# Relation rows made in a pipeline of two groups, all ahead of the carry of the spread attention sums

## The reference

```python
x = _layernorm(x + _L0_gnn_ref(x, src, dst), axis=-1)
x = _layernorm(x + _L1_gnn_ref(x, edge_index, L1_gnn_w, ...), axis=-1)
x = _layernorm(x + _L2_gnn_ref(x, ..., src, dst, edge_type_86), axis=-1)
x = _layernorm(x + _L3_gnn_ref(x, edge_weight, edge_index, 100000), axis=-1)
```

```python
c = w_comp[etype]                       # 86 x 16, one row per edge
xb = jnp.einsum('ei,bio->ebo', x, weight)
msg = jnp.einsum('eb,ebo->eo', c, xb)
y_hat = y @ A2_w.T + A2_b + rel_emb[etype]   # 86 x 32, one row per edge
```

## Time and profile before

| | us |
|---|---|
| median of 3 runs | 2744.0 |
| lowest, highest | 2743.14, 2745.68 |
| the profiled execution | 2745.77 |
| its span in the trace | 2744.0 |

### The profile page before, as it was taken

How to read it: one execution, slowest core, us unless ns; L and a number is a source line. 1 busy time by engine, 2 the same in 40 slices (tenths; PEclk the granted TensorE clock), 3 DMA queues, 4 the chain that set the end, 5 groups by cost and what they waited for, 6 DMA issues and landing times.

```text
span 2744.0 us, 24747 instructions
## 1 busy us (share of the span) xinstructions
PE 533.3 (19%) x3579; PEld 337.4 (12%) x3579; DVE 1927.4 (70%) x3512; ACT 625.0 (23%) x1417; POOL 1732.6 (63%) x1741
## 2 busy tenths in 40 slices
PE   5770000273000000000003032320255550000000
PEld 2330000273000000000003012220122220000000
DVE  7777888888835456546898476059888887587872
ACT  7982233131000000000003013441344430100000
POOL 6777777777567665646657776670566621717776
PEclk9995555597555555555556565555565655555555
DMA  6003333100112122221231201111000001200000
GB/s 229 13 12 91 97 96 100 33 13 13 61 12 34 11 25 28 21 18 72 57 66 22 63 11 9 57 23 48 7 8 8 8 4 52 21 2 10 9 9 9
DMA packets 100894, 101.68 MB, mean 37 GB/s; under 512 B 58169, under 2 KB 92649, under 8 KB 98929
## 3 DMA queue, kind: packets, MB, share of 16 engines
q0 software_dynamic: 53664, 20.91, 8.2%
q1 hardware_dynamic: 46864, 80.15, 8.1%
q10 hardware_dynamic: 320, 0.20, 0.0%
HBM read 38.06 MB, written 60.81 MB: 36 GB/s over the span
## 4 chain that ended last, share of the span: by engine, by line
DVE 36%; issue 21%; POOL 15%; DMA 9%; PE 6%; DVEq 3%; ACT 2%; ACTq 1%; POOLq 1%; SPq 0%
POOL ring L781 6%; POOL cring L477 3%; POOL out_dram L493 3%; DMA cring<-sums_by_list,cidx 2%; PE banks L2746 1%; POOL ring L874 1%; POOL attention_by_edge L881 1%; DVE RB L1259 1%; DVE banks L1100 1%; DVE banks L1090 1%; DVE SW L1096 1%; DVE SW L1095 1%; DVE SW L1105 1%; DVE SW L1383 1%; DVE banks L1084 1%
## 5 line engine op out<-in xcount | busy, mean ns | idle before, releaser
L493 POOL DMA_INDIRECT out_dram<-ring,ridx x196 | 210.3, 1073 | 128.5 <-DVE ridx L2214 68.4
L502 POOL DMA_INDIRECT XS<-in_x_dram,xsi x196 | 199.3, 1017 | 70.0 <-issue 62.2
L502 POOL DMA_INDIRECT SW<-node_table,srci x196 | 200.4, 1022 | 66.1 <-issue 66.1
L502 POOL DMA_INDIRECT XD<-in_x_dram,xdi x196 | 195.4, 997 | 62.7 <-issue 62.7
L900 POOL DMA_INDIRECT out_dram<-z4w,oidx x112 | 111.9, 999 | 126.8 <-ACT oidx L2467 98.1
L477 POOL DMA_INDIRECT cring<-sums_by_list,cidx x128 | 123.8, 967 | 101.7 <-issue 71.0
L2614 PE MATMUL banks<-tl,dcar 128*128 128x32 f32 (+1 forms) x14 | 4.4, 405 | 766.6 <-DVEq L1372 584.1
L2532 PE MATMUL banks<-YW 128*128 128x392 f16 x784 | 139.5, 331 | 46.1 <-ACT YW L2298 45.9
L781 POOL DMA_INDIRECT ring<-x_by_edge,aidx x96 | 102.3, 1066 | 49.6 <-issue 44.8
L781 POOL DMA_INDIRECT ring<-rgcn_table,aidx x56 | 61.8, 1103 | 109.6 <-DMA aidx<-rows 93.4
L2273 ACT ACT_TABLE_LOAD x22 | 28.2, 1283 | 399.7 <-DVEq L1060 399.7
(11 more groups left out here) (614 smaller groups left out, 3328.6 us busy)
## 6 DMA issues: line engine op xcount, KB each, us to landing
SW<-in_x_dram SPq DMA_DIRECT2D x20, 625.0 KB
out_dram<-SW SPq DMA_DIRECT2D x20, 625.0 KB
sums_by_list<-RB SPq DMA_DIRECT2D x2, 1800.0 KB
sums_by_edge<-RB SPq DMA_DIRECT2D x1, 3528.0 KB, 9.8
sums_by_list<-RB SPq DMA_DIRECT2D x2, 1600.0 KB
XS<-in_x_dram,xsi POOLq DMA_INDIRECT x196
list_values_by_edge<-RB SPq DMA_DIRECT2D x1, 3136.0 KB
attention_by_edge<-RB SPq DMA_DIRECT2D x1, 3136.0 KB
```

Source lines behind the costliest of these rows:

```text
L493: pool.indirect_dma_start(out=table, out_offset=off, in_=ring_row(h, j, w), in_offset=None, bounds_check=limit, oob_is_err=False).then_inc ...
L502: pool.indirect_dma_start(out=dest[:, t * w:(t + 1) * w], out_offset=None, in_=table, in_offset=bass.IndirectOffsetOnAxis(ap=idx[:, t:t + ...
```

## The change

The step of a row is cut in three on ACT (distances, one-hots, copy) and in two on PE (transposes, products). `bank[0]` and `bank[1]` are used by halves, one for even and one for odd groups, and the distances get a second buffer, `xs16[:, 0, :]`; there is still one `ohr`. PE makes the transposes of group g + 1 ahead of the products of group g; they wait for the distances of group g, the products for one-hots g and copy g - 1. ACT does distances g + 1, copy g, one-hots g + 1. Each loop now holds two groups, so that the halves are constants. The batches on PE are 8 rows, `scar`, 8 rows, `sbak`, 32 rows and the products of the last, `dbak`; nothing stands behind `dbak`.

```diff
-        off16, ohr = x16[:, 0, :], x16[:, 1, :].bitcast(BF16)
+        off16, ohr = (x16[:, 0, :], xs16[:, 0, :]), x16[:, 1, :].bitcast(BF16)
...
-        ROWS_AHEAD, ROWS_BEHIND = 4, 10
+        ROWS_AHEAD = 8
...
+        types_of = lambda b: bank[0][:, b * 256:(b + 1) * 256].bitcast(F16)
+        rows_of = lambda b: bank[1][:, b * 256:b * 256 + GT * RW]
...
-            with act.Fori(0, NG) as g:
-                relation_row(g)
+            row_distances(0, 0)
+            row_onehots(0, 0)
+            with act.Fori(0, NG // 2) as m:
+                for b in range(2):
+                    row_distances(m * 2 + (b + 1), 1 - b)
+                    row_copy(m * 2 + b, b)
+                    row_onehots(m * 2 + (b + 1), 1 - b)
+            row_copy(NG - 1, 0)
...
+            def row_types(g, b):
+
+                pe.wait_ge(s_rab, g + 0)
...
+            def row_products(g, b):
+
+                pe.wait_ge(s_rcp, g + 1)
+                pe.wait_ge(s_roh, g + 1)
...
+            def row_pairs(first, n):
+
+                with pe.Fori(0, n // 2) as m:
+                    for b in range(2):
+                        row_types(m * 2 + (first + b + 1), 1 - b)
+                        row_products(m * 2 + (first + b), b)
...
-            for link in (scar, sbak):
-                with pe.Fori(0, ROWS_AHEAD) as g:
-                    relation_row(g + (0 if link is scar else ROWS_AHEAD))
-                carry(link, D)
-            with pe.Fori(0, NG - 2 * ROWS_AHEAD - ROWS_BEHIND) as g:
-                relation_row(g + 2 * ROWS_AHEAD)
-            carry(dbak, D)
-            with pe.Fori(0, ROWS_BEHIND) as g:
-                relation_row(g + (NG - ROWS_BEHIND))
+            for k, link in enumerate((scar, sbak)):
+                row_pairs(ROWS_AHEAD * k, ROWS_AHEAD)
+                carry(link, D)
+            row_pairs(2 * ROWS_AHEAD, NG - 1 - 2 * ROWS_AHEAD)
+            row_products(NG - 1, 0)
+            carry(dbak, D)
```

More of the change, by code:

```diff
@@ L446, in load_edges @@
             queue.dma_start(tile[P - 1:P, 0:LASTV], edges_last(a)).then_inc(loaded, 16)
+        types_of = lambda b: bank[0][:, b * 256:(b + 1) * 256].bitcast(F16)
+        rows_of = lambda b: bank[1][:, b * 256:b * 256 + GT * RW]
+        assert ROWS_AHEAD % 2 == 0 and NG % 2 == 1
         def slot_count(n, i, h):
@@ L2443, in _, with row_distances, row_onehots, row_copy @@
                     A.activation(xt[:, b, :], bank[b][:, 0:P], ACT.Copy).then_inc(s_dxtc, 1)
-            def relation_row(g):
+            def row_distances(g, b):
                 act.wait_ge(s_ret, g + 1)
                 act.sem_inc(tick, 1)
-                A.activation(off16[:, :], bank[0][:, 0:256].bitcast(F16), ACT.Abs, bias=pneg[:, 0:1]).then_inc(s_rab, 1)
+                A.activation(off16[b], types_of(b), ACT.Abs, bias=pneg[:, 0:1]).then_inc(s_rab, 1)
+            def row_onehots(g, b):
                 act.wait_ge(s_rab, g + 1)
                 act.sem_inc(tick, 1)
-                A.activation(ohr[:, :], off16[:, :], ACT.Relu, scale=-1.0, bias=1.0).then_inc(s_roh, 1)
+                A.activation(ohr[:, :], off16[b], ACT.Relu, scale=-1.0, bias=1.0).then_inc(s_roh, 1)
+            def row_copy(g, b):
                 act.wait_ge(s_rmm, g + 1)
                 act.sem_inc(tick, 1)
-                A.activation(RB[:, bass.ds(g * (GT * RW), GT * RW)], bank[1][:, 0:GT * RW], ACT.Copy).then_inc(s_rcp, 1)
-            with act.Fori(0, NG) as g:
-                relation_row(g)
+                A.activation(RB[:, bass.ds(g * (GT * RW), GT * RW)], rows_of(b), ACT.Copy).then_inc(s_rcp, 1)
+            row_distances(0, 0)
[6 more added lines that the diff above has]
+            row_copy(NG - 1, 0)
             sq_2 = (sq_p[:, 0:RC * D], nxs[0][:, 0:RC * D])
@@ L2689, in _ @@
             pe.sem_inc(s_rcp, 1)
-            def relation_row(g):
-                pe.wait_ge(s_rcp, g + 1)
+            def row_types(g, b):
+                pe.wait_ge(s_rab, g + 0)
                 pe.sem_inc(tick, 1)
                 for c in range(GT):
-                    last = M.transpose(bank[0][:, 0:256].bitcast(F16)[:, c * P:(c + 1) * P],
+                    last = M.transpose(types_of(b)[:, c * P:(c + 1) * P],
                                        ety16[:, bass.ds(g * GT + c, 1)].to_broadcast([P, P]), ident_h[:, :])
                 last.then_inc(s_ret, 1)
+            def row_products(g, b):
+                pe.wait_ge(s_rcp, g + 1)
                 pe.wait_ge(s_roh, g + 1)
@@ L2700, in relation_row @@
                     for k in range(3):
-                        last = M.matmul(bank[1][:, c * RW:(c + 1) * RW], ohr[:, c * P:(c + 1) * P], rel3[:, k, :],
+                        last = M.matmul(rows_of(b)[:, c * RW:(c + 1) * RW], ohr[:, c * P:(c + 1) * P], rel3[:, k, :],
                                         start=k == 0, stop=k == 2)
                 last.then_inc(s_rmm, 1)
-            for link in (scar, sbak):
-                with pe.Fori(0, ROWS_AHEAD) as g:
-                    relation_row(g + (0 if link is scar else ROWS_AHEAD))
+            def row_pairs(first, n):
[3 more added lines that the diff above has]
+                        row_products(m * 2 + (first + b), b)
+            for c in range(GT):
+                last = M.transpose(types_of(0)[:, c * P:(c + 1) * P], ety16[:, c:c + 1].to_broadcast([P, P]),
+                                   ident_h[:, :])
+            last.then_inc(s_ret, 1)
+            for k, link in enumerate((scar, sbak)):
+                row_pairs(ROWS_AHEAD * k, ROWS_AHEAD)
                 carry(link, D)
-            with pe.Fori(0, NG - 2 * ROWS_AHEAD - ROWS_BEHIND) as g:
-                relation_row(g + 2 * ROWS_AHEAD)
+            row_pairs(2 * ROWS_AHEAD, NG - 1 - 2 * ROWS_AHEAD)
+            row_products(NG - 1, 0)
             carry(dbak, D)
-            with pe.Fori(0, ROWS_BEHIND) as g:
-                relation_row(g + (NG - ROWS_BEHIND))
             pe.wait_ge(s_grp, 1)
```

## The result

| | before | changed |
|---|---|---|
| median us | 2744.1 | 2718.4 |
| lowest, highest | 2743.14, 2745.68 | 2716.25, 2721.93 |
| the profiled execution, and its span | 2745.77, 2744.0 | 2721.93, 2720.1 |

The ratio is 0.9907, with a 95% interval of 0.989 to 0.9924. The forecast was 2718.2 in a range of 2715 to 2725: right, and the profiled execution, forecast at 2720.0, took 2721.9. The kernel before was run once more beside the changed one, which makes its median 2744.1 instead of 2744.0.

The account below looks back on a forecast made before the run. The prediction took DVE's 26.9 us wait for ACT's square, late behind the last ten serial rows, as the bound. -26.8 + 1.0 = -25.8 us gave 2718.2 against the median 2744.0 (2720.0 profiled), range 2715 to 2725.

Parts of the forecast that it names:

- The sum: Whole kernel: 26.8 us gained at a DVE wait, 1.0 lost at a new one, together -25.8 us.
- The stall: DVE's wait at L1493 for ACT's square of XD: goes, moving L1493 from 1849.11 to 1822.33, 26.8 us gained.
- The pipeline: Rows on PE and ACT: overlapped, 2.0 us a row, between bounds of 1.68 and the serial 3.87.
- The path I had drawn: Between two products: issue 0.14, products 0.65, hand-over 0.18, copy 0.34, one-hots 0.64, together 1.95 us.
- The first two batches: PE ahead of the first two carries: 8 rows each instead of 4, at a cost of nothing.
- The scatters: POOL beside DVE's norm of XD: one scatter blocked at each of five addition pairs, some 4.3 us; at most 11.
- The wait for the table: Start of the norm of XS: the attention table lands 1.0 us after DVE wants it.
- Behind 1892: Relation groups and the rest to the end: all shifts with DVE, groups keep 308 us, change taken as 0.
- the rival that the gain would not reach the end: Behind the norms: a later stage has a start of its own, 2728 to 2744 us; chance 0.04.
- The table comes later: Start of the norm of XS: 3 to 7 us of gain go into a DVE wait, 2721 to 2726; chance 0.10.
- No overlap: Rows on PE and ACT: stay at 3.87 us, third carry 15.1 late, 2732 us; chance 0.05.
- Slower: Rows on PE and ACT: round grows to 4.45 us, third carry 42.9 late, 2760 us; chance 0.03.

Follow-up runs that it names:

- ahead_16: The changed kernel with batches of 16 rows instead of 8 ahead of the first and of the second carry; 2717.0 us, ratio 0.9903.
- ahead_20: The changed kernel with batches of 20 rows instead of 8 ahead of the first and of the second carry; 2728.4 us, ratio 0.9944.
- psum_adds: The changed kernel with both additions per chunk in the norm of XD reading a zeroed PSUM tile, so the layer is not computed; 2716.7 us, ratio 0.9897.
- order_only_8: The kernel before with its serial rows, 8, 8 and 33 of them, all ahead of the third carry; 2732.3 us, ratio 0.9958.
- pipe_only: The changed kernel with four rows ahead of each of the first two carries and the last eleven products behind the third; 2722.2 us, ratio 0.9917.

## Why the prediction was right, point by point

**The sum.** Forecast 25.8 us less, measured 25.7 by the medians and 25.9 by the two stretches, neither of them good to better than 2 us, so the closeness itself is luck. The two waits give 25.15, since the table is waited for 0.75 longer than forecast. What makes it up is 0.7 ahead of the third carry, for which the prediction had no term: the load of the attention sums landed after 10.3 us in this profile and after 11.0 in the one before, which is as much.

**The stall.** Forecast: the 26.8 us wait of L1493 goes whole. The row is gone, and the norm of XD runs as if ACT had never been late. The last copy now comes at about 1744, far ahead of the square. Right.

**The pipeline.** Forecast 2.0 us a row, bounds 1.68 and 3.87; measured 1.78, from the products of the third batch ((1743.44 - 1686.38) / 32). The path I had drawn is the one that sets it, but two of its terms were too long. Timelines of PE and ACT in the changed kernel, one round, to be held against the earlier trace rows:

```profile
1688.16 0.64 PE L2722 MATMUL banks<-rel,xw 128*128 128x48 bf16 x12
...
1689.00 0.33 ACT L2465 ACTIVATE RB<-banks 128x192 f32 x1
1689.22 0.62 ACT L2459 ACTIVATE xw<-xw 128x512 bf16<-128x512 f16 x1
...
1689.94 0.64 PE L2722 MATMUL banks<-rel,xw 128*128 128x48 bf16 x12
```

Products 0.64, hand-over 0.20, one-hots 0.22 behind the start of the copy where I had counted its 0.34, one-hots 0.62, and 0.10 instead of 0.14 until the products. ACT starts an activation ahead of the end of the one before, if nothing holds it; in the earlier trace rows the copy of 0.33 and the square stand 0.23 apart in the same way, and I read that row without drawing on it. ACT has 0.3 us idle in each round, so it is not the bound; and as its activations overlap, the 1.68 that I had called the least possible was no floor. The miss cost nothing: PE idles 66.65 us ahead of the third carry, where I had 59.

**The first two batches.** Forecast: no cost, with DVE's spreading less than half of the 24 us to SP's first staging. Measured: DVE is done at 1695.85, 10.5 behind the second carry, and 13.8 are left. PE still idles 4.55 and 13.20 us ahead of the carries. Right, and `ahead_16` and `ahead_20` put the slack where it belongs.

**The scatters.** Forecast: one held up for each pair of additions, 4.3 us in all, so that the load is issued 46.6 us behind the third carry (1851.78 + 4.3 - 1809.5). Measured: five of 1.69 to 1.89, 4.35 more than five of 0.98, and 1857.34 - 1810.73 = 46.6. Right. POOL's lines and SP's issue with its landing, against the earlier trace rows:

```profile
1825.08 1.69 POOL L802 DMA_INDIRECT attention_table<-ring,aidx  x1 [0.31 <-DMA ring<-YW]
...
1854.25 1.89 POOL L802 DMA_INDIRECT attention_table<-ring,aidx  x1 [0.30 <-issue]
...
1857.34 0.35 SPq L725 DMA_DIRECT2D YW<-attention_table  x1
...
YW<-attention_table SPq DMA_DIRECT2D x1, 3136.0 KB, 10.6
```

**The wait for the table.** Forecast 1.0, measured 1.75: the term that was mis-sized. The load took 10.6 us where the earlier trace rows have 10.0, which is 0.6 of the 0.75; the rest is the 0.1 from its landing to DVE's start, and rounding; over the runs that load it whole it took 10.0 to 10.8. By the accounting of the prediction the lengthened scatters are what puts DVE behind the table at all, and `psum_adds` showed that without them there is no wait.

The Trainium skill, "SBUF — State Buffer", section "Who interferes with whom", was named in the prediction for the rule that a DVE instruction with two SBUF inputs contends with a GpSimd instruction that reads SBUF. `psum_adds` agrees, if the issue of a scatter is such an instruction: with one input in PSUM the scatters beside the additions take 0.98 again. The other half, that DVE waits in turn for a GpSimd instruction that came first, is not seen in the additions of the changed kernel, which take 1.09 also where a scatter was under way as they began, as at 1814.35 and 1815.47. It does show elsewhere in the same trace, in a cast of one input. All engines of the changed kernel: of two casts that start under one scatter the first takes 0.17, and the second 0.44, until the scatter ends at 1699.35.

```profile
1698.32 1.03 POOL L885 DMA_INDIRECT attention_by_edge<-ring,aidx  x1 [0.30 <-issue]
1698.49 0.17 DVE L2100 CAST dneg<-tl 32x32 bf16<-32x32 f32 x1
...
1698.91 0.44 DVE L2100 CAST dneg<-tl 32x32 bf16<-32x32 f32 x1
```

The prediction took the additions alone, and for them its reading held: no term of the sum moved.

**Behind 1892.** Forecast: all shifts with DVE, and the groups keep their 308 us and their clock. The same window as in the earlier trace rows, placed 26 us earlier: busy us of each engine, granted clock 0.58 against 0.59, so the same mixture of 1.2 and 2.4 GHz.

```profile
1934.00:2242.00 308.00, 168.44 (x784) 87.44 (x784) 262.88 (x349) 122.93 (x456) 169.69 (x173) 0.58 0.03 7
```

The stretch behind the third carry lost 25.1 us where the two waits account for 25.15, so the rival that the gain would not reach the end falls, to within the 2 us by which that stretch varies.

**The rivals.** "The table comes later": it came 1.75 late, in my own case and not in the 3 to 7 of the rival. "No overlap" was the time of `order_only_8`, 2732, and not of the change. "Slower" decides from 4.11 us a row on; the row takes 1.78.

## What to carry to other kernels

A serial ring between two in-order engines (3.87 us here) cost nothing here until an instruction that somebody waits for was queued behind it; then both the length of the ring and its place in the queue counted (of 26 us the shorter ring alone brought some 20, the new place alone 11.4 in one placement and a loss of 5.7 in another). Before filling idle time ahead of a hand-over, ask who takes the result next and when: 10 us of delay at both carries were free here, because SP took the sums 13.8 us after they were ready. And when a wait is removed, walk the engine that fetches the next input against the one that now arrives earlier; where its load is needed chunk by chunk, cut the load at the first chunks.

## What the runs showed of the hardware

- An indirect DMA issue on POOL of 0.98 us takes 1.69 to 1.89 when it starts under a DVE addition of two SBUF tiles, and 0.98 under one that reads PSUM for one of them. Held ones end some 0.85 behind the end of the first addition, and the second, with the bias, did not hold them again. A bias addition can hold one as well, if the scatter starts under it: in `pipe_only` three take 1.82 to 1.89 so.
- An addition of two SBUF tiles is not the only thing that holds a scatter: in `psum_adds` one that starts 0.09 behind a TENSOR_SCALAR of one input (L1413, 0.31 us) takes 1.08 and ends 0.86 behind its end; the kernel before has the same at 1809.18.
- The other way round DVE is held too, if seldom: the cast above takes 0.44 instead of 0.17, one in `ahead_16` 0.40 (at 1703.12), each until the scatter under way ends. An addition in `pipe_only` that starts 0.01 ahead of a scatter takes 1.14 instead of 1.09 (at 1827.82).
- POOL and DVE fall into step by this. In the changed kernel two pairs of additions are 7.34 us apart, five scatters with what stands between them 6.43; the held one makes up the missing 0.91, so that from 1832 on each pair meets a scatter 0.05 to 0.06 behind its start.
- Activations that wait for nothing start ahead of the end of the last: in the changed kernel 0.22 behind the start of a copy of 0.33.
- A load cut in two on one queue: the first piece lands after 3.7 us with 448 KB and 4.7 with 896 KB, the second piece, issued 0.4 later, 10.2 and 10.3 after its own issue. Both are there 10.6 to 10.7 us behind the first issue, no later than the undivided 3136 KB (10.0 to 10.8).
- With nothing changed ahead of the rows, the third carry stood at 1805.8 in `pipe_only`, 1810.7 in the changed kernel and 1812.9 in the same kernel on another chip; the first products already stood that far apart (1634.9, 1640.4, 1642.4). The stretch from the first products to it is 170.4 to 170.9 in the six profiles of changed or partly changed kernels that do not touch what sets it, and 171.1 before. The stretch behind it is less steady: 909.4 and 909.7 in the two profiles of the changed kernel, 907.6 and 907.4 in `ahead_16` and `ahead_20`, which have the same wait of 1.8 for the table. What makes up these 2 us stays open, and for that reason I take no gain under 2 us from this stretch alone.
